# FP4 feed-forward in a four-layer kernel: levels from the rounded bit pattern, the sign put back as a bit

## The chip, the cores and the metric

One Trainium2 chip; the program runs on 1 of its cores. The metric is the device time of one execution in microseconds (us), as the median over several executions.

## The reference, cut to what matters

The whole program is four transformer-like layers, each with an attention-like stage and a feed-forward stage, on 16 sequences of 256 tokens with 128 features. The change touches only the feed-forward stage of the first layer, where tokens, weights and the gated hidden values are quantized to FP4 and back, in blocks of 16 along the last dimension:

```python
def fp4_quant_dequant(x):
    """Blockwise FP4 (E2M1) quantize + dequantize along the last dim."""
    shape = x.shape
    xb = x.reshape(shape[:-1] + (shape[-1] // BLOCK, BLOCK))
    scale = jnp.max(jnp.abs(xb), axis=-1, keepdims=True) / 6.0
    scale = jnp.maximum(scale, jnp.float32(1e-12))
    xn = xb / scale
    idx = jnp.searchsorted(_MID, jnp.abs(xn))
    q = _GRID[idx] * jnp.sign(xn) * scale
    return q.reshape(shape)
```

`_GRID` is 0, 0.5, 1, 1.5, 2, 3, 4, 6 and `_MID` holds the seven midpoints 0.25, 0.75, 1.25, 1.75, 2.5, 3.5, 5. Around it stand a layer norm with modulation, the products with `w_gate`, `w_up` (352 by 128) and `w_down` (128 by 352), a SiLU, and a gated residual.

## The kernel before, in words

`build_program` runs ten stages one after the other, with a barrier between them: a load, `stage_mamba`, `stage_fp4_ffn`, six further stages, and a store. All engines execute instruction lists written out by hand; semaphores join them.

`stage_fp4_ffn` works on B = 16 items, one sequence of 256 tokens each. It first normalizes all of x in 8 steps of two sequences (`AdaNorm`: TensorE centres and averages, ScalarE squares and takes the logarithm and exponential, VectorE multiplies, L287, and modulates, L290). Between these steps VectorE quantizes all weights in one go (`weight_step`; the quantizer `qw`, 128 by 1120 elements): it issues one piece of the work before each normalization step, and what is left after the eighth. TensorE then turns the weights, and the items follow.

There are three quantizers: `qw` for the weights, `qx` for the tokens of an item (128 by 256) and `qh` for its gated hidden values (128 by 704). In each, `Quantizer.act` (ScalarE) makes `mag` with Abs (L707) and `sign` with Sign (L708); `Quantizer.pool` (GpSimd) multiplies `sign` by half the block's scale (L714); and `Quantizer.dve` (VectorE) takes the block maximum (L732), scale, half scale and reciprocal (L734 to L736), normalizes `mag` by a product with the reciprocal, which is broadcast over the 16 elements of a block (L738), and counts the midpoints that are exceeded, in nine instructions (L741 to L753). The product of level and signed half scale (L758) is the result. `done` puts a semaphore wait behind every step that the next one reads; L734 and L735 and the reciprocal have no wait between L735 and L736.

The order of VectorE for item n is written in `item`: `hidden(n)` (gate by up, L990), `quantize_tokens(n + 1)`, `residual(n - 1)` (L298) and `quantize_hidden(n)`. TensorE does `back(n - 1)` (six transposes of the quantized hidden values, L896, between which ScalarE copies, L956, and six products with `w_down`, L901), then `project(n + 1)` (L881, L887, L888), then the transpose of the tokens of n + 2 (L859). ScalarE copies, quantizes its part and applies SiLU (L950). GpSimd copies the normalized tokens of n + 2 to a fixed place (`fixed`, L834) and makes the two products of L714. `residual(n - 1)` waits for `back(n - 1)`, and `back(n - 1)` waits for `quantize_hidden(n - 1)`, the last thing of the item before.

Of the kernel before, what the change touches and what calls it, by code (L numbers as in the profile page):

```python
# [8 lines left out]
P = 128  # L9
ALU = mybir.AluOpType  # L10
# [4 lines left out]
I32 = mybir.dt.int32  # L15
# [669 lines left out]
class Quantizer:  # L685
# [4 lines left out]
    STEPS = 11  # L690

    def __init__(self, core, sb, sg, name, blocks):
        self.nc, self.sg, self.name = core.nc, sg, name
        self.amax = sb(name + "_amax", [P, blocks, 1])
        self.scale = sb(name + "_scale", [P, blocks, 1])
        self.half = sb(name + "_half", [P, blocks, 1])
        self.mag = sb(name + "_mag", [P, blocks, 16])
        self.sign = sb(name + "_sign", [P, blocks, 16])
        self.level = sb(name + "_level", [P, blocks, 16])
        self.blocks = blocks  # L700

    def act(self, act, n, src, ready):

        nc, sg, name = self.nc, self.sg, self.name
        act.wait_ge(ready, n + 1)
        wait(act, sg[name + "_done"], n)
        nc.scalar.activation(self.mag[:, :, :], src, ACT.Abs).then_inc(sg[name + "_mag"], 1)  # L707
        nc.scalar.activation(self.sign[:, :, :], src, ACT.Sign).then_inc(sg[name + "_sign"], 1)  # L708

    def pool(self, pool, n):  # L710
        sg, name = self.sg, self.name
        pool.wait_ge(sg[name + "_sign"], n + 1)
        pool.wait_ge(sg[name + "_half"], n + 1)
        pool.tensor_tensor(self.sign[:, :, :], self.sign[:, :, :], self.half[:, :, :].to_broadcast([P, self.blocks, 16]),  # L714
                           ALU.mult).then_inc(sg[name + "_signed"], 1)

    def dve(self, dve, n, src, dst, read=0):
# [18 lines left out]
        done(nc.vector.reciprocal(self.amax[:, :, :], self.scale[:, :, :]))  # L736
# [3 lines left out]
        dve.wait_ge(sg[name + "_half"], n + 1)  # L740
        done(nc.vector.tensor_scalar(flat(self.level), flat(self.mag), 5.0, 2.0, ALU.is_gt, ALU.mult))  # L741
        yield
        for mid in (3.5, 2.5):
            done(nc.vector.scalar_tensor_tensor(out=flat(self.level), in0=flat(self.mag), scalar=mid, in1=flat(self.level),
                                                op0=ALU.is_gt, op1=ALU.add))
            yield
        done(nc.vector.tensor_scalar(flat(self.level), flat(self.level), 2.0, None, ALU.mult))
        yield
        for mid in (1.75, 1.25, 0.75):
            done(nc.vector.scalar_tensor_tensor(out=flat(self.level), in0=flat(self.mag), scalar=mid, in1=flat(self.level),  # L750
                                                op0=ALU.is_gt, op1=ALU.add))
            yield
        nc.vector.scalar_tensor_tensor(out=flat(self.level), in0=flat(self.mag), scalar=0.25, in1=flat(self.level),  # L753
                                       op0=ALU.is_gt, op1=ALU.add).then_inc(sg[name + "_level"], 1)
        dve.wait_ge(sg[name + "_level"], n + 1)
        dve.wait_ge(sg[name + "_signed"], n + 1)
        wait(dve, sg[name + "_taken"], read)
        nc.vector.tensor_tensor(dst, self.level[:, :, :], self.sign[:, :, :], ALU.mult).then_inc(sg[name + "_done"], 1)  # L758
# [3 lines left out]
def stage_fp4_ffn(core, T):  # L762
# [7 lines left out]
    with ExitStack() as ctx:  # L770
# [56 lines left out]
        def _(pool):  # L827
# [8 lines left out]
            def first():  # L836
                qw.pool(pool, 0)
                pool.wait_ge(sg["h"], B // 2)
                fixed(0, 0)
                fixed(1, 1)  # L840
                qx.pool(pool, 0)

            def item(n, j, nxt=2):
                if nxt == 2:
                    fixed(n + 2, j)
                if nxt:
                    qx.pool(pool, n + 1)
                qh.pool(pool, n)
# [131 lines left out]
        def _(dve):  # L980
# [6 lines left out]
            def hidden(n):  # L987
                dve.wait_ge(sg["silu"], n + 1)
                wait(dve, sg["qh_sign"], n)
# [2377 lines left out]
```

## Time and profile before

| What | us |
|---|---|
| three runs, median (lowest to highest) | 5523.27 (5519.79 to 5526.17) |
| the profiled execution's own time | 5521.02 |
| its span in the profile | 5519.3 |
| VectorE busy in the span | 3922.5 (71%) |
| TensorE busy in the span | 4929.2 (89%) |
| GpSimd busy in the span | 2660.5 (48%) |
| ScalarE busy in the span | 3359.4 (61%) |

The profile is one execution, with its instructions timed engine by engine. Its span lies 1.7 us under the time of its own execution, and that one 2.3 us under the median. The feed-forward stage that the change touches lies between about 563 and 919 us of the span. An average over the span tells nothing of it; the stage has to be read alone.

### The profile page before, as it was taken

The numbers are of one execution on the slowest core, as the hardware profiler recorded it, in microseconds if no ns is written. First come the engines' busy times: TensorE is split into PE (matmuls) and PEld (weight loads), VectorE is DVE, ScalarE is ACT, GpSimd is POOL, SyncE is SP. The second block draws the span as 40 slices with busy tenths as digits, with TensorE's granted clock in tenths as the row PEclk, the third lists the DMA queues.
The fourth block names the chain that finished last, engine by engine and source line by source line (L and its number), as shares of the span: only waits on it lengthen the run. The fifth ranks groups of instructions, "written<-read, shape, count | busy, mean of one in ns | idle before, by whom it ended". The sixth has DMA issues, their size and how long they took to land. (4 is left out here: it accounts for less than half of the span.)

```text
span 5519.3 us, 130512 instructions
## 1 busy us (share of the span) xinstructions
PE 4929.2 (89%) x50569; PEld 3352.3 (61%) x50569; DVE 3922.5 (71%) x6510; ACT 3359.4 (61%) x5923; POOL 2660.5 (48%) x1681
## 2 busy tenths in 40 slices
PE   6888555997899999999999999999999999799897
PEld 4444233554677667776777677766776777566544
DVE  5999797775677777777777677767777777477553
ACT  5776322554666666666666666666666666455444
POOL 4777110000566556665666566655555666266200
PEclk8999656998999999999999999999999999899898
DMA  2121000000000100010000000010001000000020
GB/s 84 61 77 62 4 0 7 2 1 19 17 12 12 29 14 11 11 30 15 11 11 20 25 11 11 12 30 12 11 11 33 12 11 11 14 2 2 24 62 19
DMA packets 76242, 113.90 MB, mean 21 GB/s; under 512 B 22496, under 2 KB 53424, under 8 KB 72048
## 3 DMA queue, kind: packets, MB, share of 16 engines
q1 hardware_dynamic: 67744, 110.60, 7.3%
q8 instruction: 157, 2.57, 0.2%
q10 hardware_dynamic: 8256, 0.03, 0.1%
q14 instruction: 85, 0.70, 0.0%
HBM read 70.38 MB, written 2.49 MB: 13 GB/s over the span
## 5 line engine op out<-in xcount | busy, mean ns | idle before, releaser
L2211 POOL TENSOR_TENSOR lt_qk<-lt_qk,lt_rot 128x1024 f32<-128x1024 f32 x384 | 907.0, 2362 | 207.3 <-DVE lt_rot L2575 207.3
L2221 POOL TENSOR_TENSOR lt_prob<-lt_prob,lt_total 128x1024 f32<-128x1024 f32 x192 | 365.1, 1902 | 1086.5 <-DVE lt_total L2597 1086.5
L2216 POOL TENSOR_TENSOR lt_qk<-lt_qk,lt_rnorm 128x1024 f32<-128x1024 f32 x384 | 726.2, 1901 | 110.5 <-ACT lt_rnorm L2451 102.9
L2258 PE MATMUL lt_ps<-lt_w_qk,lt_xs 128*128 128x512 f32 x1536 | 749.8, 611 | 23.0 <-DMA lt_scales<-in_L_scales 11.3
L2310 PE MATMUL lt_ps<-lt_z,lt_fold 128*128 128x256 f32 x3072 | 678.8, 379 | 1.3 <-ACT lt_z L2479 1.3
L2310 PEld LDWEIGHTS lt_ps<-lt_z,lt_fold 128*128 128x128 f32 x3072 | 583.6, 190 | 121.5 <-ACT lt_z L2479 24.4
L2572 DVE TENSOR_TENSOR lt_qk<-lt_ps,lt_table 128x1024 f32<-128x1024 f32 x384 | 467.8, 1218 | 79.0 <-ACT lt_sq L2441 72.1
L2575 DVE TENSOR_TENSOR lt_rot<-lt_ps,lt_table 128x512 f32<-128x512 f32 x768 | 490.1, 679 | 0.0
L2587 DVE TENSOR_REDUCE lt_nmax<-lt_ps 128x16 f32<-128x1024 f32 x192 | 229.9, 1197 | 360.5 <-PE lt_ps L2278 360.4
L2582 DVE TENSOR_REDUCE lt_norm<-lt_sq 128x16 f32<-128x1024 f32 x384 | 463.4, 1207 | 0.0
L2258 PEld LDWEIGHTS lt_ps<-lt_w_qk,lt_xs 128*128 128x128 f32 x1536 | 272.7, 193 | 253.9 <-issue 247.2
L2441 ACT ACTIVATE lt_sq<-lt_ps 128x1024 f32<-128x1024 f32 x384 | 393.2, 1024 | 50.9 <-PE lt_ps L2258 44.3
L2301 PEld LDWEIGHTS lt_ps<-lt_probT,lt_xw 64*128 64x128 f32 x3072 | 295.7, 187 | 175.2 <-issue 87.1
L2462 ACT ACTIVATE lt_prob<-lt_prob 128x1024 f32<-128x1024 f32 x192 | 203.2, 1058 | 320.2 <-DVE lt_prob L2590 320.2
L2265 PE MATMUL lt_ps<-ident,lt_qk 128*128 128x128 f32 x3072 | 389.9, 275 | 8.8 <-DVE lt_rot L2575 7.9
L2301 PE MATMUL lt_ps<-lt_probT,lt_xw 64*128 64x256 f32 x3072 | 385.1, 389 | 12.6 <-ACT lt_probT L2467 3.4
L2479 ACT COPY lt_z<-lt_ps 128x1024 f32<-128x1024 f32 x384 | 380.1, 1016 | 22.9 <-PE lt_ps L2301 21.7
L2265 PEld LDWEIGHTS lt_ps<-ident,lt_qk 128*128 128x128 f32 x3072 | 348.2, 142 | 37.8 <-DVE lt_rot L2575 8.8
L2846 POOL TENSOR_TENSOR mb_drive<-mb_u,mb_bs 128x1024 f32<-128x1024 f32 x128 | 301.2, 2359 | 84.6 <-DVE mb_state L3057 79.2
L3057 DVE TENSOR_TENSOR_SCAN mb_state<-mb_decay,mb_drive 128x1024 f32<-128x1024 f32 x128 | 292.2, 2283 | 20.4 <-POOL mb_drive L2846 19.3
L2278 PE MATMUL lt_ps<-lt_kT,lt_qT 64*32 64x64 f32 x24576 | 287.6, 225 | 14.3 <-issue 14.3
L2278 PEld LDWEIGHTS lt_ps<-lt_kT,lt_qT 64*32 64x32 f32 x24576 | 254.9, 105 | 59.5 <-issue 59.5
(406 smaller groups left out, 9935.5 us busy)
## 6 DMA issues: line engine op xcount, KB each, us to landing
mb_bs<-mb_rows SPq DMA_DIRECT2D x16, 1536.0 KB, 7.6
lt_xw<-lt_xw SPq DMA_DIRECT2D x192, 128.0 KB, 2.3
mb_bs<-mb_rows SPq DMA_DIRECT2D x16, 512.0 KB, 4.2
mo_gate_b<-mo_rows SPq DMA_DIRECT2D x16, 512.0 KB, 5.5
lt_xs<-h SPq DMA_DIRECT2D x96, 64.0 KB, 1.9
lt_w_qk<-in_L_ffn_Wqkv SPq DMA_DIRECT2D x6, 1024.0 KB, 4.9
lt_xs<-h SPq DMA_DIRECT2D x96, 63.8 KB, 1.9
lt_wvT<-in_L_wvT SPq DMA_DIRECT2D x6, 512.0 KB, 7.4
```

The costliest lines, as they stand in the source:

```text
L2211: pool.tensor_tensor(qk[:, u, :, :], qk[:, u, :, :], rot[:, u % 2, :, :], ALU.add).then_inc(sg["added"], 1)
L2216: pool.tensor_tensor(qk[:, u, :, :], qk[:, u, :, :], rnorm[:, u, :, :].to_broadcast([P, H, DH]), ALU.mult).then_inc(sg["qk"], 1)
L2258: last = pe.matmul(AT[u][:, 512 * k:512 * k + 512], xs[:, m.j, c:c + P], w_qk[:, a, 512 * k:512 * k + 512], start=True, stop=True)
L2265: last = pe.transpose(to[:, P * g:P * g + P], qk[:, u, 2 * g:2 * g + 2, :].rearrange("p a b -> p (a b)"), core.ident[:, :])
L2278: last = pe.matmul(to[WIN * w:WIN * w + WIN, 512 * k + 64 * g:512 * k + 64 * g + 64], qT[r:r + 64, g, c:c + WIN], kT[r:r + 64, g, c:c + 2 ...
L2301: last = pe.matmul(to[:, c:c + 256], xw[r:r + 64, copy, i_w, :], probT[r:r + 64, t, :, WIN * w:WIN * w + WIN], start=True, stop=True, tile ...
L2310: last = pe.matmul(attn, fold[:, slot // 8, slot % 8, :], z[:, k, :, i, :], start=(slot == 0), stop=(slot == H - 1))
L2441: nc.scalar.activation(sq[:, u % 2, :], AT[u], ACT.Square).then_inc(sg["square"], 1)
L2479: act.copy(dst, src.rearrange("p (k c) -> p k c", k=2)).then_inc(sg["z"], 1)
L2572: nc.vector.tensor_tensor(qk[:, u, :, :], src, table[:, t, a, 0, :, :].to_broadcast([P, H, DH]), ALU.mult)
L2575: last = nc.vector.tensor_tensor(rot[:, u % 2, :, HD * k:HD * k + HD], src[:, :, HD * (1 - k):HD * (1 - k) + HD], table[:, t, a, 1, :, HD ...
L2582: nc.vector.tensor_reduce(norm[:, u, :], sq[:, u % 2, :].rearrange("p (h d) -> p h d", h=H), AX.X, ALU.add).then_inc(sg["sumsq"], 1)
```

## The change

The quantizer works out the same values in another way. Sign on ScalarE (L708) and the product on GpSimd (L714) are gone, and with them the tile `sign`. VectorE divides by half the scale instead of the scale, for which the reciprocal now waits for the half. It finds the level by cutting the exponent out of the bit pattern (a bitwise AND on an int32 view), adding a quarter of it to the value, and cutting the sum to its upper bits (a second AND); two comparisons give the correction for the small levels. The level is then multiplied by the half scale, broadcast over the block, and the last instruction takes the sign bit of the source with AND and joins it with OR. This last instruction reads the source, so `hidden(n)` now waits until `quantize_hidden(n - 1)` is done, where it waited for the Sign of ScalarE. A new tile `low` takes the place of `sign`.

```diff
-    STEPS = 11
+    STEPS = 10
...
-        nc.scalar.activation(self.sign[:, :, :], src, ACT.Sign).then_inc(sg[name + "_sign"], 1)
-
-    def pool(self, pool, n):
-        sg, name = self.sg, self.name
-        pool.wait_ge(sg[name + "_sign"], n + 1)
-        pool.wait_ge(sg[name + "_half"], n + 1)
-        pool.tensor_tensor(self.sign[:, :, :], self.sign[:, :, :], self.half[:, :, :].to_broadcast([P, self.blocks, 16]),
-                           ALU.mult).then_inc(sg[name + "_signed"], 1)
...
         nc.vector.tensor_scalar(self.half[:, :, :], self.scale[:, :, :], 0.5, None, ALU.mult).then_inc(sg[name + "_half"], 1)
-        done(nc.vector.reciprocal(self.amax[:, :, :], self.scale[:, :, :]))
+        dve.wait_ge(sg[name + "_half"], n + 1)
+        done(nc.vector.reciprocal(self.amax[:, :, :], self.half[:, :, :]))
         dve.wait_ge(sg[name + "_mag"], n + 1)
         done(nc.vector.tensor_tensor(self.mag[:, :, :], self.mag[:, :, :], self.amax[:, :, :].to_broadcast(shape), ALU.mult))
         yield
-        dve.wait_ge(sg[name + "_half"], n + 1)
-        done(nc.vector.tensor_scalar(flat(self.level), flat(self.mag), 5.0, 2.0, ALU.is_gt, ALU.mult))
+        bits = flat(self.level).bitcast(I32)
+        done(nc.vector.tensor_scalar(bits, flat(self.mag).bitcast(I32), 0x7F800000, None, ALU.bitwise_and))
         yield
-        for mid in (3.5, 2.5):
-            done(nc.vector.scalar_tensor_tensor(out=flat(self.level), in0=flat(self.mag), scalar=mid, in1=flat(self.level),
-                                                op0=ALU.is_gt, op1=ALU.add))
-            yield
-        done(nc.vector.tensor_scalar(flat(self.level), flat(self.level), 2.0, None, ALU.mult))
+        done(nc.vector.scalar_tensor_tensor(out=flat(self.level), in0=flat(self.level), scalar=0.25 - 2.0 ** -23, in1=flat(self.mag),
+                                            op0=ALU.mult, op1=ALU.add))
         yield
-        for mid in (1.75, 1.25, 0.75):
-            done(nc.vector.scalar_tensor_tensor(out=flat(self.level), in0=flat(self.mag), scalar=mid, in1=flat(self.level),
-                                                op0=ALU.is_gt, op1=ALU.add))
-            yield
-        nc.vector.scalar_tensor_tensor(out=flat(self.level), in0=flat(self.mag), scalar=0.25, in1=flat(self.level),
-                                       op0=ALU.is_gt, op1=ALU.add).then_inc(sg[name + "_level"], 1)
+        done(nc.vector.tensor_scalar(bits, bits, 0x7FC00000, None, ALU.bitwise_and))
+        yield
+        done(nc.vector.tensor_scalar(flat(self.low), flat(self.mag), 1.5, -2.0, ALU.is_gt, ALU.add))
+        yield
+        done(nc.vector.scalar_tensor_tensor(out=flat(self.low), in0=flat(self.mag), scalar=0.5, in1=flat(self.low),
+                                            op0=ALU.is_gt, op1=ALU.add))
+        yield
+        nc.vector.scalar_tensor_tensor(out=flat(self.level), in0=flat(self.level), scalar=2.0, in1=flat(self.low),
+                                       op0=ALU.max, op1=ALU.add).then_inc(sg[name + "_level"], 1)
         dve.wait_ge(sg[name + "_level"], n + 1)
-        dve.wait_ge(sg[name + "_signed"], n + 1)
+        done(nc.vector.tensor_tensor(self.level[:, :, :], self.level[:, :, :], self.half[:, :, :].to_broadcast(shape), ALU.mult))
+        yield
         wait(dve, sg[name + "_taken"], read)
-        nc.vector.tensor_tensor(dst, self.level[:, :, :], self.sign[:, :, :], ALU.mult).then_inc(sg[name + "_done"], 1)
+        nc.vector.scalar_tensor_tensor(out=dst.bitcast(I32), in0=src.bitcast(I32), scalar=-2 ** 31, in1=self.level[:, :, :].bitcast(I32),
+                                       op0=ALU.bitwise_and, op1=ALU.bitwise_or).then_inc(sg[name + "_done"], 1)
...
             def first():
-                qw.pool(pool, 0)
                 pool.wait_ge(sg["h"], B // 2)
                 fixed(0, 0)
                 fixed(1, 1)
-                qx.pool(pool, 0)
 
             def item(n, j, nxt=2):
                 if nxt == 2:
                     fixed(n + 2, j)
-                if nxt:
-                    qx.pool(pool, n + 1)
-                qh.pool(pool, n)
...
-                wait(dve, sg["qh_sign"], n)
+                wait(dve, sg["qh_done"], n)
                 nc.vector.tensor_tensor(hid[:, :, :], gate[:, :, :], ps_u[:, :, 0:I], ALU.mult).then_inc(sg["hid"], 1)
```

The pieces of the weight quantizer are fewer now, and one more of them falls between the normalization steps. VectorE at the end of the normalization, before the change (L750, L753 and L758 are pieces of `qw`, L287 and L290 the last normalization steps):

```order
191 L287 TENSOR_TENSOR h<-cen,rstd 128x512
192 L290 TENSOR_SCALAR h<-h,mod 128x256 x2
193 L750 SCALAR_TENSOR_TENSOR fp_qw_level<-fp_qw_mag,fp_qw_level 128x1120
194 L287 TENSOR_TENSOR h<-cen,rstd 128x512
195 L290 TENSOR_SCALAR h<-h,mod 128x256 x2
196 L750 SCALAR_TENSOR_TENSOR fp_qw_level<-fp_qw_mag,fp_qw_level 128x1120
197 L753 SCALAR_TENSOR_TENSOR fp_qw_level<-fp_qw_mag,fp_qw_level 128x1120
198 L758 TENSOR_TENSOR fp_wraw<-fp_qw_level,fp_qw_sign 128x1120
```

And the same place with the change, with the changed kernel's own line numbers:

```order
191 L287 TENSOR_TENSOR h<-cen,rstd 128x512
192 L290 TENSOR_SCALAR h<-h,mod 128x256 x2
193 L746 SCALAR_TENSOR_TENSOR fp_qw_level<-fp_qw_level,fp_qw_low 128x1120
194 L749 TENSOR_TENSOR fp_qw_level<-fp_qw_level,fp_qw_half 128x1120
195 L287 TENSOR_TENSOR h<-cen,rstd 128x512
196 L290 TENSOR_SCALAR h<-h,mod 128x256 x2
197 L752 SCALAR_TENSOR_TENSOR fp_wraw<-fp_wraw,fp_qw_level 128x1120
198 L724 TENSOR_REDUCE fp_qx_amax<-fp_h_tok 128x16
```

Behind the last normalization step three pieces of `qw` stood; one stands there now.

## Rows read from the trace of the kernel before

**Rows 1.** Stretch, busy us of PE, PEld, DVE, ACT, POOL; granted clock, DMA

```profile
617.20:892.60 275.40, 149.57 (x346) 80.91 (x346) 259.02 (x450) 67.83 (x147) 43.10 (x43) 0.62 0.00 0
```

**Rows 2.** VectorE in order of time, one item: start us, us, engine, line, operation

```profile
707.82 0.89 DVE L758 TENSOR_TENSOR fp_hidq<-fp_qh_level,fp_qh_sign 128x704 f32<-128x704 f32 x1
...
714.75 0.42 DVE L758 TENSOR_TENSOR fp_hq<-fp_qx_level,fp_qx_sign 128x256 f32<-128x256 f32 x1
715.31 0.48 DVE L298 SCALAR_TENSOR_TENSOR x<-fp_ps_o,mod,x 128x256 f32 x1
...
716.85 0.18 DVE L735 TENSOR_SCALAR fp_qh_half<-fp_qh_scale 128x44 f32<-128x44 f32 x1
716.94 0.42 DVE L736 RECIPROCAL fp_qh_amax<-fp_qh_scale 128x44 f32<-128x44 f32 x1
717.40 1.91 DVE L738 TENSOR_TENSOR fp_qh_mag<-fp_qh_mag,fp_qh_amax 128x704 f32<-128x704 f32 x1
...
726.19 0.89 DVE L758 TENSOR_TENSOR fp_hidq<-fp_qh_level,fp_qh_sign 128x704 f32<-128x704 f32 x1
```

**Rows 3.** One group of VectorE: duration ns min/median/max, first and last start us

```profile
L758 DVE TENSOR_TENSOR fp_hidq<-fp_qh_level,fp_qh_sign x16: 891/892/893, 634.0 to 909.9; 128x704 f32<-128x704 f32 x16
```

**Rows 4.** TensorE in order of time, the same item

```profile
708.77 0.69 PE L896 MATMUL fp_ps_t<-ident,fp_hidq 128*128 128x128 f32 x2 [6.26 <-DVE fp_hidq L758]
...
712.19 2.93 PE L901 MATMUL fp_ps_o<-fp_hidT,fp_wd 128*128 128x256 f32 x6 [0.46 <-ACT fp_hidT L956]
```

**Rows 5.** Who waited for whom, VectorE, 604 to 920 us: in total, times, longest

```profile
DVE x L298 <- PE fp_ps_o L901: 13.8, 8, 6.5
```

**Rows 6.** ScalarE in order of time: the SiLU of the next item

```profile
721.48 0.76 ACT L950 ACTIVATE fp_gate<-fp_ps_g 128x704 f32<-128x704 f32 x1 [5.15 <-PE fp_ps_u L888]
```

**Rows 7.** Groups of VectorE by form: count, busy us, mean ns, idle before

```profile
L750 DVE SCALAR_TENSOR_TENSOR fp_qh_level<-fp_qh_mag,fp_qh_level 128x704 f32<-128x704 f32 x48 | 42.8, 892 | 1.6
...
L738 DVE TENSOR_TENSOR fp_qh_mag<-fp_qh_mag,fp_qh_amax 128x704 f32<-128x704 f32 x16 | 30.5, 1908 | 0.5
...
L738 DVE TENSOR_TENSOR fp_qx_mag<-fp_qx_mag,fp_qx_amax 128x256 f32<-128x256 f32 x16 | 13.7, 857 | 0.5
...
L741 DVE TENSOR_SCALAR fp_qh_level<-fp_qh_mag 128x704 f32<-128x704 f32 x16 | 9.4, 587 | 0.6
...
L747 DVE TENSOR_SCALAR fp_qh_level<-fp_qh_level 128x704 f32<-128x704 f32 x16 | 8.4, 527 | 0.5
...
L753 DVE SCALAR_TENSOR_TENSOR fp_qx_level<-fp_qx_mag,fp_qx_level 128x256 f32<-128x256 f32 x16 | 6.8, 426 | 0.6
...
L750 DVE SCALAR_TENSOR_TENSOR fp_qw_level<-fp_qw_mag,fp_qw_level 128x1120 f32<-128x1120 f32 x3 | 3.9, 1316 | 0.0
...
L738 DVE TENSOR_TENSOR fp_qw_mag<-fp_qw_mag,fp_qw_amax 128x1120 f32<-128x1120 f32 x1 | 2.9, 2896 | 0.0
...
L741 DVE TENSOR_SCALAR fp_qw_level<-fp_qw_mag 128x1120 f32<-128x1120 f32 x1 | 0.7, 735 | 0.0
```

**Rows 8.** GpSimd in order of time, beside L738 of rows 2

```profile
717.17 1.38 POOL L714 TENSOR_TENSOR fp_qh_sign<-fp_qh_sign,fp_qh_half 128x704 f32<-128x704 f32 x1 [6.15 <-DVE fp_qh_half L735]
```

**Rows 9.** A group of VectorE with a broadcast operand in a later stage

```profile
L2590 DVE TENSOR_TENSOR lt_prob<-lt_ps,lt_nmax 128x1024 f32<-128x1024 f32 x192 | 235.0, 1224 | 14.1
```

**Rows 10.** All engines, normalization and weights, in order of time

```profile
570.99 1.12 ACT L708 ACTIVATE fp_qw_sign<-fp_wraw 128x1120 f32<-128x1120 f32 x1
...
577.64 0.69 DVE L287 TENSOR_TENSOR h<-cen,rstd 128x512 f32<-128x512 f32 x1 [6.37 <-ACT rstd L278]
...
600.40 2.86 POOL L834 COPY fp_h_fixed<-h 128x256 f32<-128x256 f32 x2 [18.71 <-DVE h L290]
...
604.36 0.41 DVE L732 TENSOR_REDUCE fp_qx_amax<-fp_h_tok 128x16 f32<-128x256 f32 x1
```

**Rows 11.** Groups of GpSimd by form: the copy of the tokens, here and in a later stage

```profile
L834 POOL COPY fp_h_fixed<-h 128x256 f32 x12 | 12.7, 1060 | 0.0
...
L1839 POOL COPY ca_h_fixed<-h 128x256 f32 x14 | 5.6, 400 | 40.6 <-PE ca_ps_s L1866 40.6
```

More of the change, by code:

```diff
@@ L697, in __init__ @@
         self.mag = sb(name + "_mag", [P, blocks, 16])
-        self.sign = sb(name + "_sign", [P, blocks, 16])
         self.level = sb(name + "_level", [P, blocks, 16])
+        self.low = sb(name + "_low", [P, blocks, 16])
         self.blocks = blocks
```

## The prediction

> **What bounds the kernel now.** The change lies in one stage, so I read that stretch alone. First the busy times by stretch: over items 0 to 14 (617.2 to 892.6 us) VectorE is busy 259.0 of 275.4 us (94%), TensorE 54%, ScalarE 25%, GpSimd 16%, and TensorE's granted clock is 0.62, which means most of the time its lower level (1.2 of 2.4 GHz) [rows 1]. VectorE is the bound, nearly. Then the order of time of one item, to see how near. Call t the end of the quantized hidden values (L758, 707.82 + 0.89 = 708.71). The next such end is at 727.08, so an item takes 18.37 us; over all 16 items the mean is the same, 275.9 us in 15 periods, 18.39 [rows 3]. Inside it VectorE finishes the tokens of the next item at 715.17 and starts the residual (L298) at 715.31, t + 6.60; from there to the end of the hidden values it needs 11.77 [rows 2]. TensorE meanwhile starts its transposes at 708.77, and the last product that the residual reads ends at 712.19 + 2.93 = 715.12, t + 6.41 [rows 4]. So both inputs of the residual arrive within 0.05 us of each other. The waits show the same from the other side: in 8 cases the residual waited for that product, at most 6.5 us [rows 5]. This is the number that decides most: what VectorE saves **before** the residual runs into TensorE's chain, which hangs on t too; what it saves **behind** it shortens every item. SiLU of the next item ends at 722.24, 4.8 us before VectorE wants it [rows 6], so the chain through the gate has room.
>
> **Prices.** A VectorE instruction with two tensor inputs costs 892 ns at 704 elements, 426 at 256, 1316 at 1120; one with a single input costs 527 at 704 and 735 at 1120 [rows 7], and about 293 at 256 by the same line (157 ns and two elements per cycle of 0.96 GHz). The product L738 stands out: 1908, 857 and 2896 ns. That looks like the price of its broadcast operand, but isn't. GpSimd's product runs from 717.17 to 718.55 and L738 from 717.40 to 719.31 [rows 2, 8]; from the end of GpSimd's to that of VectorE's are 0.76 us, and 704 elements at one per cycle are 0.73. VectorE stood still until GpSimd was through. And a broadcast operand with no GpSimd beside it costs 1224 ns for 1024 elements, one element per cycle and 157 ns [rows 9]. So without L714 the product L738 should cost 892, 426 and 1316, and the added product with the half scale the same.
>
> **Hidden values, behind the residual.** Before, from L738 to the result: 1908 + 2 x 527 + 7 x 892 = 9206 ns (L738, two single-input steps, seven with two). After: 892 (L738) + 3 x 527 (two ANDs and one comparison) + 3 x 892 + 892 (broadcast product) + 892 (sign) = 6933. That is 2.27 less, and one instruction less takes its gap of 0.04 with it. The reciprocal now waits for the half: it started 0.09 us after the start of the half and 0.09 before its end; behind a wait the next instruction starts 0.04 after the end (L736 to L738) [rows 2], so this costs 0.13. Net 2.18 us per item, all 16 items: **34.9 us**. The Trainium skill, "VectorE: DVE Perf Modes", section on the DRAIN, says that a semaphore after each operation costs nothing extra; by it the sum would gain 2.1 us. The rows show an overlap that the wait takes away, and I go by them.
>
> **Tokens, ahead of the residual.** Before 857 + 2 x 293 + 7 x 426 = 4425, after 426 + 3 x 293 + 5 x 426 = 3435; with the gap and the wait 0.99 + 0.04 - 0.12 = 0.91 us less. `hidden` now waits for the end of L758, where it could overlap it, for another 0.12 at most. In items 1 to 15 all of this is worth nothing: VectorE would be ready at about t + 5.8, TensorE's product is not there before t + 6.4, and the residual starts at t + 6.6 as before. The saving becomes a wait of some 0.8 us. Only the tokens of item 0 and those of item 1, in front of which no residual stands, count: **1.8 us**.
>
> **Normalization and weights.** ScalarE's Sign of the weights (1.12 us) lies ahead of its part of the normalization, for which VectorE idles 6.37 us until 577.64 [rows 10]: 1.1 us earlier. From there VectorE is nearly full. Its weight work falls by 1.58 (L738 without GpSimd), and behind it from 2 x 735 + 7 x 1316 = 10.68 to 3 x 735 + 5 x 1316 = 8.79 us, with 0.13 for the reciprocal's wait and 0.04 for the gap: 3.4 us. Of these 4.5 us I count 3.6: the tokens of item 0 hang on a GpSimd copy and a transpose behind the last normalization step, and the copy that started at 600.40 and the one behind it took 2.86 us beside VectorE [rows 10]. **3.6 us.**
>
> **At nothing.** ScalarE's two Signs per item: ScalarE is busy a quarter of the time and the Abs that VectorE reads comes well before. GpSimd's two products: nobody waits for them but VectorE; the copy of the tokens loses its place behind them and comes earlier. It took 1060 ns here and 400 in a later stage [rows 11], as it waits for VectorE, while the VectorE step behind it was 0.06 us longer than its like (587 against 527) [rows 7]; I keep that cost as it is, at another step. The Trainium skill, "SBUF — State Buffer", section on the two sides, has a lock: whichever of GpSimd and such a VectorE instruction starts first holds the ports for all of it. If the copy won each time, VectorE would stand up to 0.4 us in 16 items instead of 0.06, and the sum would be 5 us worse; the rows show the copy as the one that waits.
>
> **Sum.** 34.9 + 1.8 + 3.6 = 40.3 us. The profiled execution took 5521.0, so 5480.7; the median of the runs is 2.3 above it: **5483**.
>
> **Open prices.** No row shows a bitwise instruction. The two ANDs are bounded below by 527 and above by 892, the price of one element per cycle; I take 527, since they are of the form of L741 and L747 (one tensor in SBUF, an immediate). At 892 the hidden values lose 0.73 per item (11.7 us), weights and first tokens 1.7 more. The sign instruction reads two tensors like L750, 892; I find no reason for less. All three could also be slower than any row, which is rival C.
>
> **Rivals.**
>
> A. *The ANDs run at one element per cycle.* For it: nothing shows integer data at two per cycle. Against: the form of the instruction. 5483 + 13.4 = 5496. By the Trainium skill, "Vector Engine (DVE) Microarchitecture Reference", section on performance modes, the two-port mode depends on SBUF and an even size, not on type, which speaks for 527.
>
> B. *TensorE's chain gets shorter too.* The items come closer, TensorE's share rises from 54% to about 62%, and if its granted clock were at the upper level during L896 and L901, the residual would wait no more and the 0.9 us of the tokens would count in 14 items: 12.6 us more, 5470. Against: the granted clock of 0.62 [rows 1], and that in this chain of transposes, copies and products nothing gets denser. The Trainium skill, "TensorE: Matmul & The Clock Gate", part 1, has the clock rise with TensorE's recent activity, which is this rival's mechanism.
>
> C. *Slower: bitwise instructions on 32-bit integers take two cycles per element.* Then an AND of 704 costs 1624 ns and the sign 1624: 2.93 us more per item, 46.8 in 16; in the tokens 1.07, of which the wait of 0.9 hides most (about 4 us in all), and in the weights 4.7. That is 55.6 over the forecast: 5539, slower by 15 us. It decides from about 1.7 cycles per element on, where the extra cost reaches 40 us. Against: no instruction of VectorE in this profile is that slow once GpSimd's share is taken out.
>
> D. *The broadcast costs double in itself* and the overlap with GpSimd is chance. Then L738 stays at 1908 and the new product costs 1908 too: 0.15 us per item, with the weights some 4 us in all: 5519, no change. The change would then have saved GpSimd's work and nothing else. Against: the broadcast product that stands alone [rows 9], and how exactly the ends fit.
>
> **Chances.** Forecast 0.70, A 0.12, B 0.10, C 0.05, D 0.03. A measurement of this kernel tells 0.2%, 11 us, from no change: forecast, A and B are faster (0.92), D the same (0.03), C slower (0.05). The range reaches from B to A with a few us for the clock's phase in the stages behind, which run the same work at other moments: 5467 to 5502. C and D are left out, with 0.08.
>
> **What would show it.** L738 at 892, 426 and 1317 ns; the ANDs at 527 and 293; the two products with a broadcast alike; a period of about 16.2 us; the residual waiting for TensorE in nearly every item, 0.6 to 0.9 us each, with L298 still at t + 6.6; the first tokens' reduction (604.36 before [rows 10]) 3 to 4.5 us earlier. The forecast is wrong if L738 is still near 1900, if an AND costs more than 900, or if the residual starts well before t + 6.4.

## The result and the profile after

| What | before | after |
|---|---|---|
| median of the runs side by side, 4 of each (us) | 5521.53 | 5470.35 |
| lowest to highest | 5517.36 to 5526.17 | 5467.04 to 5471.46 |
| ratio of the times | | 0.991 (0.9895 to 0.9925) |
| the profiled execution, own time and span | 5521.02, 5519.3 | 5470.79, 5469.0 |
| feed-forward stage | 347.32 | 307.07 |
| next two stages | 429.4 | 429.1 |
| local transformer stage | 3433.8 | 3422.8 |
| everything behind it | 738.8 | 739.4 |

The time fell by 51 us to 5470.35, inside the range (5467 to 5502), 13 below the predicted 5483. The lower half of the table cuts the span at fixed instructions of the program: the stage runs from the start of VectorE's reduction of the weights to the start of its last residual, the local transformer from one of GpSimd's fills at its beginning (`lt_kT`) to one at the beginning of the next stage (`gq_nmax`). The changed stage gave 40.25 us, against 40.3 forecast. Another 11.0 came from the local transformer, whose code is the same.

First the busy times of the changed kernel by stretch, the columns as in [rows 1]. The stretch is 15 periods of 16.17 us:

```profile
615.00:857.50 242.50, 144.06 (x350) 81.48 (x350) 214.48 (x419) 53.01 (x117) 8.17 (x12) 0.64 0.00 0
```

VectorE is busy 88% of it, where it was 94% [rows 1]; GpSimd's 43.10 us have become 8.17. TensorE's granted clock is 0.64 after 0.62. That is a mean over everything TensorE does there; in the chain that the residual waits for it is lower, as the next views show.

VectorE in order of time, one item (start us, us, engine, line, operation, idle time before it and what ended it):

```profile
692.10 0.89 DVE L752 SCALAR_TENSOR_TENSOR fp_hidq<-fp_hid,fp_qh_level 128x704 int32<-128x704 int32 x1
693.10 0.89 DVE L980 TENSOR_TENSOR fp_hid<-fp_gate,fp_ps_u 128x704 f32<-128x704 f32 x1
...
698.34 0.43 DVE L752 SCALAR_TENSOR_TENSOR fp_hq<-fp_h_tok,fp_qx_level 128x256 int32<-128x256 int32 x1
699.60 0.48 DVE L298 SCALAR_TENSOR_TENSOR x<-fp_ps_o,mod,x 128x256 f32 x1 [0.84 <-PE fp_ps_o L891]
...
701.13 0.19 DVE L727 TENSOR_SCALAR fp_qh_half<-fp_qh_scale 128x44 f32<-128x44 f32 x1
701.35 0.43 DVE L729 RECIPROCAL fp_qh_amax<-fp_qh_half 128x44 f32<-128x44 f32 x1
701.81 0.89 DVE L731 TENSOR_TENSOR fp_qh_mag<-fp_qh_mag,fp_qh_amax 128x704 f32<-128x704 f32 x1
702.74 0.53 DVE L734 TENSOR_SCALAR fp_qh_level<-fp_qh_mag 128x704 int32<-128x704 int32 x1
...
708.29 0.89 DVE L752 SCALAR_TENSOR_TENSOR fp_hidq<-fp_hid,fp_qh_level 128x704 int32<-128x704 int32 x1
```

The quantized hidden values are ready at 692.99 and again at 709.18. The residual L298 starts at 699.60, 6.61 us after the first, as before [rows 2], though the tokens are now done at 698.77. From the residual to the result it is 9.58 us, where it was 11.77. TensorE's part hangs on the same event and kept its length:

```profile
693.05 0.69 PE L886 MATMUL fp_ps_t<-ident,fp_hidq 128*128 128x128 f32 x2 [4.24 <-DVE fp_hidq L752]
...
696.47 2.93 PE L891 MATMUL fp_ps_o<-fp_hidT,fp_wd 128*128 128x256 f32 x6 [0.46 <-ACT fp_hidT L946]
```

The last product ends at 699.40, 6.41 after the result, the same number as in [rows 4]. The closer items did not bring TensorE's upper level (2.4 GHz) to this chain: its granted clock is 0.50 here (first row below, columns as in [rows 1]), the lower level. Behind the very first result, at 628.68, it was 0.61 (second row); there the chain took 5.91 us and the residual started 5.95 after the result.

```profile
692.99:699.40 6.41, 4.97 (x13) 3.06 (x14) 5.26 (x15) 1.80 (x4) 0.00 (x0) 0.50 0.00 0
628.68:634.60 5.92, 4.49 (x13) 2.59 (x14) 5.25 (x14) 1.80 (x4) 0.00 (x0) 0.61 0.00 0
```

What VectorE saved ahead of the residual has become idle time (who waited for whom, VectorE, 590 to 880 us):

```profile
DVE x L298 <- PE fp_ps_o L891: 23.8, 16, 6.5
```

Of these 23.8 us the residuals of the last two items hold 12.0, where they held 12.2 of the 13.8 before [rows 5]; the new waiting lies in the other items.

The groups of VectorE by form give the prices (count, busy us, mean ns, idle before), to be held against [rows 7]:

```profile
L746 DVE SCALAR_TENSOR_TENSOR fp_qh_level<-fp_qh_level,fp_qh_low 128x704 f32<-128x704 f32 x16 | 14.6, 915 | 0.5
...
L749 DVE TENSOR_TENSOR fp_qh_level<-fp_qh_level,fp_qh_half 128x704 f32<-128x704 f32 x16 | 14.3, 896 | 0.5
L752 DVE SCALAR_TENSOR_TENSOR fp_hidq<-fp_hid,fp_qh_level 128x704 int32<-128x704 int32 x16 | 14.3, 892 | 1.7
L731 DVE TENSOR_TENSOR fp_qh_mag<-fp_qh_mag,fp_qh_amax 128x704 f32<-128x704 f32 x16 | 14.3, 892 | 0.6
...
L739 DVE TENSOR_SCALAR fp_qh_level<-fp_qh_level 128x704 int32<-128x704 int32 x16 | 8.6, 536 | 0.5
...
L734 DVE TENSOR_SCALAR fp_qh_level<-fp_qh_mag 128x704 int32<-128x704 int32 x16 | 8.4, 527 | 0.5
```

The product with the reciprocal fell from 1908 to 892 ns in the same form; what changed beside it is GpSimd's product, which is gone. The first experiment puts that back. The ANDs L734 and L739 cost what one tensor and an immediate cost in float: with 293 ns at 256 elements (measured below) they take 0.52 ns per element, half the 1.04 of an instruction with two tensors (892 and 425). The integer AND-OR L752 costs what any instruction with two tensors costs.

### The profile page after: what moved, and what is told of

Same layout as the page of the kernel before. It is cut to its first block and busy times, and to the rows that moved or that the text cites. A ratio compares the mean times of both kernels' runs of the same rounds, so it can differ in the third digit from the quotient of the medians.

```text
span 5469.0 us, 130315 instructions
## 1 busy us (share of the span) xinstructions
PE 4913.4 (90%) x50569; PEld 3348.9 (61%) x50569; DVE 3873.2 (71%) x6477; ACT 3344.0 (61%) x5890; POOL 2620.7 (48%) x1648
## 5 line engine op out<-in xcount | busy, mean ns | idle before, releaser
L2248 PE MATMUL lt_ps<-lt_w_qk,lt_xs 128*128 128x512 f32 x1536 | 744.6, 608 | 21.6 <-DMA lt_scales<-in_L_scales 11.8
L2291 PE MATMUL lt_ps<-lt_probT,lt_xw 64*128 64x256 f32 x3072 | 383.6, 388 | 11.8 <-ACT lt_probT L2457 2.3
```

What stands on the lines that cost most here:

```text
L2248: last = pe.matmul(AT[u][:, 512 * k:512 * k + 512], xs[:, m.j, c:c + P], w_qk[:, a, 512 * k:512 * k + 512], start=True, stop=True)
L2291: last = pe.matmul(to[:, c:c + 256], xw[r:r + 64, copy, i_w, :], probT[r:r + 64, t, :, WIN * w:WIN * w + WIN], start=True, stop=True, tile ...
```

## The experiments

All of them start from the changed kernel, unless said otherwise. Period means the mean distance between quantized hidden values over 15 items; the stage is measured as in the table. Where no number of runs is given, the stage and period are of the one profiled run. Repeats stand beside their first run.

### The product back on GpSimd, on a tile that nobody reads

Is it GpSimd that made the product with the reciprocal slow? GpSimd multiplies an otherwise unused tile by the half scale, at the old places; VectorE's last instruction also waits for it.

```diff
+        self.aside = sb(name + "_aside", [P, blocks, 16])
...
+        pool.wait_ge(sg[name + "_half"], n + 1)
...
+        pool.tensor_tensor(self.aside[:, :, :], self.aside[:, :, :], self.half[:, :, :].to_broadcast([P, self.blocks, 16]),
+                           ALU.mult).then_inc(sg[name + "_signed"], 1)
```

> The changed kernel, with GpSimd's products put back on a tile of their own that nobody uses (same sizes, same wait for the half scale, VectorE's last instruction waits for them). Lock theory: the product L738/L731 of VectorE, which starts 0.2 us behind GpSimd's, stands still until that ends, so it is back at about 1908, 857 and 2896 ns where it is 892, 425 and 1326 in the changed kernel; all else of VectorE stays. The stage (first reduction of the weights to the last residual, 307.1 us in the changed kernel, 347.3 before) gets 16 x 1.02 + 2 x 0.43 + 1.6 = 19 us longer, 326 us. Rival, the product was dear for another reason (its place, its operands): it stays at 892 and the stage at 307.

Measured: stage 324.29 us (+17.2), period 17.07; the one run took 5498.78. GpSimd and then VectorE at the place in question, two views of one stretch:

```profile
707.76 1.38 POOL L715 TENSOR_TENSOR fp_qh_aside<-fp_qh_aside,fp_qh_half 128x704 f32<-128x704 f32 x1 [5.97 <-issue]
```

```profile
707.66 0.43 DVE L738 RECIPROCAL fp_qh_amax<-fp_qh_half 128x44 f32<-128x44 f32 x1
708.12 1.77 DVE L740 TENSOR_TENSOR fp_qh_mag<-fp_qh_mag,fp_qh_amax 128x704 f32<-128x704 f32 x1
```

GpSimd ends at 709.14, VectorE's product at 709.89: 0.75 us later, the time that 704 elements take at 1.04 ns each (0.73 us), though it started at 708.12. So the product's data moved only after GpSimd had ended. The mean is 1769 ns, not 1908, because the reciprocal's wait starts it 0.36 us behind GpSimd and not 0.23; that is the miss of about 2 us against the expectation.

The repeat, timed in 4 runs:

> e1_product_aside again, with more runs. Its stage is 17.2 us longer than the changed kernel's. If nothing else differs, its runs lie 17 us above c2_after_again within 3. In its first profile the local transformer stage took 3434.1 us, as before the change; if GpSimd's products in this stage lengthen a later one in some way, the distance is 24 us or more.

Median 5489.57, ratio to before 0.995 (0.9934 to 0.9967). That is 18.4 above the changed kernel beside it, for a stage that is 18.0 longer (324.35 against 306.39).

### GpSimd busy, but reading nothing

Against the kernel before this one, the product aside:

```diff
-        pool.tensor_tensor(self.aside[:, :, :], self.aside[:, :, :], self.half[:, :, :].to_broadcast([P, self.blocks, 16]),
-                           ALU.mult).then_inc(sg[name + "_signed"], 1)
+        pool.memset(self.aside[:, :, :], 1.0).then_inc(sg[name + "_signed"], 1)
```

> As e1_product_aside, but GpSimd only fills the unused tile with a constant at the same moment, so it writes and reads nothing. If what stops VectorE is GpSimd's reading, the products of VectorE stay at 892 and 425 ns and the stage at 307 us. If writing is enough, a fill of 704 elements (about 0.65 us by the 1031 ns for 1120) that starts 0.2 us ahead holds VectorE for some 0.45 us, the product is at 1.3 us and the stage at about 315 us.

Measured: stage 306.74, as without it (the whole run, 5480.02, is 9 us longer; 5.3 of that stand in the next two stages, with 434.4). The two engines again, GpSimd's row first:

```profile
701.49 0.68 POOL L715 MEMSET fp_qh_aside<- 128x704 f32 x1 [6.27 <-DVE fp_qh_half L735]
```

```profile
701.88 0.89 DVE L739 TENSOR_TENSOR fp_qh_mag<-fp_qh_mag,fp_qh_amax 128x704 f32<-128x704 f32 x1
```

They overlap for 0.29 us and the product takes its 0.89. So a GpSimd that is busy does not by itself hold VectorE: its product does, which reads two tiles, and its fill doesn't, which reads none. The Trainium skill, "SBUF — State Buffer", section "SBUF: two separate sides", says of a VectorE operation with two inputs in SBUF: it contends only against a GpSimd operation that reads SBUF, and the one that comes second waits for all of the first. Both runs agree; that it is the reading, and not another difference between a product and a fill, rests on that page.

### Which half of the change pays

The old levels with the new sign: seven comparisons in eight instructions as before (L741 to L753; they were counted as nine above), then the broadcast product and the sign bit on VectorE; no Sign, no GpSimd product. Against before:

```diff
-        dve.wait_ge(sg[name + "_signed"], n + 1)
+        done(nc.vector.tensor_tensor(self.level[:, :, :], self.level[:, :, :], self.half[:, :, :].to_broadcast(shape), ALU.mult))
...
-        nc.vector.tensor_tensor(dst, self.level[:, :, :], self.sign[:, :, :], ALU.mult).then_inc(sg[name + "_done"], 1)
+        nc.vector.scalar_tensor_tensor(out=dst.bitcast(I32), in0=src.bitcast(I32), scalar=-2 ** 31, in1=self.level[:, :, :].bitcast(I32),
+                                       op0=ALU.bitwise_and, op1=ALU.bitwise_or).then_inc(sg[name + "_done"], 1)
```

> The kernel before with one half of the change: no Sign, no GpSimd product; the level of nine steps as before, then VectorE multiplies it by the half scale and joins the sign bit. Theory: VectorE gets back what it stood still behind GpSimd (1908 to 892 per item) and pays it out again for its own product (892) and a further gap, and `hidden` can no longer overlap the end of the item before: the stage stays at 347 us within 2 (347.3 before), so this half is worth nothing by itself. Rival, that freeing GpSimd is what pays: the stage falls by 16 us or more, to 331 or less.

> k7_sign_only again, with more runs. Its stage is 2.5 us shorter than before the change (344.8 for 347.3). If nothing else differs its runs lie 2 to 3 us under those of the kernel before; if taking Sign and GpSimd's products away shortens the stages behind, 8 us or more under.

Measured: stage 344.83 and 344.78 us, 2.5 below before, a little more than the 2 expected; 1.1 of it lie ahead of the first tokens, where ScalarE's Sign of the weights is gone. Period 18.32. Ten runs: 5509.52, ratio 0.9982 (0.9973 to 0.9992), 10 us less than before (5519.75 beside it), of which the stage explains a quarter; the rest is taken up below.

And the new levels with the old sign (Sign on ScalarE, half scale on GpSimd, `level` by `sign` at the end):

```diff
-        done(nc.vector.tensor_tensor(self.level[:, :, :], self.level[:, :, :], self.half[:, :, :].to_broadcast(shape), ALU.mult))
...
-        nc.vector.scalar_tensor_tensor(out=dst.bitcast(I32), in0=src.bitcast(I32), scalar=-2 ** 31, in1=self.level[:, :, :].bitcast(I32),
-                                       op0=ALU.bitwise_and, op1=ALU.bitwise_or).then_inc(sg[name + "_done"], 1)
+        dve.wait_ge(sg[name + "_signed"], n + 1)
+        nc.vector.tensor_tensor(dst, self.level[:, :, :], self.sign[:, :, :], ALU.mult).then_inc(sg[name + "_done"], 1)
```

> The changed kernel with the old sign path: Sign on ScalarE and the product with the half scale on GpSimd, the new level of six steps on VectorE, and a plain product at the end. Theory: VectorE loses 0.88 us behind GpSimd in the product (1769 ns for 892, as in e1_product_aside) and saves its own product of 892: the stage stays within 1.5 us of the changed kernel's 307.1, so the shorter level is the whole gain. Rival, as in k7_sign_only: without freeing GpSimd most of the 40 us are gone again and the stage is over 320 us.

Measured: stage 307.72 us, within 0.7 of the changed kernel; the one run took 5473.64. The same view of groups, this kernel:

```profile
L740 DVE TENSOR_TENSOR fp_qh_mag<-fp_qh_mag,fp_qh_amax 128x704 f32<-128x704 f32 x16 | 28.5, 1778 | 0.6
```

VectorE pays 0.886 us here for GpSimd's company and would pay 0.892 for the broadcast product. Whatever the change says of GpSimd and Sign, nearly all of the stage's gain (39.6 of 40.25 us) is the shorter chain of levels; the product on VectorE costs as much as GpSimd's product cost VectorE.

### The residual behind the hidden values

If the tokens' saving is lost to TensorE's chain, a different order must win it back:

```diff
-                if not fresh(n):
-                    residual(n - 1)
                 quantize_hidden(n)
+                if not fresh(n):
+                    residual(n - 1)
```

> The changed kernel with the residual of item n - 1 behind the quantization of the hidden values of item n, where it stood ahead of it. Theory that TensorE's chain ahead of the residual eats what the tokens saved: the 0.8 us wait in each item goes, the period falls from 16.2 to about 15.35 us (14 items, 11 us) and in item 15 the wait of 5.5 us goes too: some 17 us in all, the stage at about 290 us and the time at about 5453. Rival, the wait is hidden behind something else that then ends last (the gate's chain over TensorE and SiLU, which is ready at t + 13.5): the period stays near 16 and at most the 5.5 us go.

Measured: stage 287.24 us (-19.8, some 17 expected), period 14.83; 5454.26 in 4 runs, ratio 0.9879 (0.9863 to 0.9896). Only the last residual still waits (VectorE, 590 to 880 us), and in the loop it stands hard against its neighbours:

```profile
DVE x L298 <- PE fp_ps_o L891: 6.1, 1, 6.1
```

```profile
702.42 0.89 DVE L752 SCALAR_TENSOR_TENSOR fp_hidq<-fp_hid,fp_qh_level 128x704 int32<-128x704 int32 x1
703.23 0.48 DVE L298 SCALAR_TENSOR_TENSOR x<-fp_ps_o,mod,x 128x256 f32 x1
703.62 0.88 DVE L980 TENSOR_TENSOR fp_hid<-fp_gate,fp_ps_u 128x704 f32<-128x704 f32 x1
```

The period shrinks by 1.34 us in the mean, unevenly. The last of the 15 distances falls by 4.4 us, from 15.92 to 11.48: its residual had waited 5.5. The other 14 fall by 1.1 each, from 16.19 to 15.07: the wait of 0.84 to 0.99 and some 0.2 of gaps, since the residual starts 0.08 before the end of L752 and L980 0.09 before the residual's. Expected were 0.8 for each of these and 5.5 for the last.

The same with the half scale computed straight from the block maximum, one small instruction fewer on the chain of each quantizer:

```diff
-        done(nc.vector.tensor_scalar(self.scale[:, :, :], self.amax[:, :, :], 1.0 / 6.0, 1e-12, ALU.mult, ALU.max))
-        nc.vector.tensor_scalar(self.half[:, :, :], self.scale[:, :, :], 0.5, None, ALU.mult).then_inc(sg[name + "_half"], 1)
+        nc.vector.tensor_scalar(self.half[:, :, :], self.amax[:, :, :], 1.0 / 12.0, 5e-13, ALU.mult, ALU.max).then_inc(sg[name + "_half"], 1)
```

> e3_residual_late, and the half scale computed straight from the block maximum (one twelfth of it, lower bound 5e-13), so that the scale's own instruction goes. VectorE ends last in every item of e3_residual_late (period 14.83 us), so each of the two instructions saved per item, 0.19 and 0.17 us with a gap of 0.04, counts in full: period 14.4, stage 287.2 - 7 = 280 us, time 34 us under c2_after_again. Rival, the gate's chain (ready 13.5 us behind the hidden values) or the Abs of ScalarE becomes what ends last: the stage stays above 284.

Measured: 5442.73 in 4 runs (5439.81 to 5446.00), ratio 0.986 (0.9844 to 0.9877): faster than both kernels, 28.5 below the changed one beside it. Expected were 34 below and a stage of 280. Stage 277.73, period 14.35, another 0.48 per item (most of it the scale with its gap, 0.22 in the hidden values and 0.21 in the tokens, which now count in every item). The stage alone gives 28.7 against the changed kernel's repeat.

### Where the other 11 us are

The stages behind differ though their code is the same. One thought was the moment at which they start; a chain of memsets ahead of the weights delays it and leaves the rest alone (32 of them here; 10 in the first try):

```diff
+            for pad in range(32):
+                pool.memset(wraw[:, :, :], 0.0).then_inc(sg["w_pad"], 1)
+                pool.wait_ge(sg["w_pad"], pad + 1)
             pool.memset(wraw[:, :, :], 0.0).then_inc(sg["w_zero"], 1)
```

> The changed kernel with ten more fills of the weight tile by GpSimd ahead of the stage's first load, each waited for: a plain delay of about 11 us, nothing else. It tells where the 11 us come from that the local transformer stage (unchanged code) is shorter with the change: 3433.7 us from its first fill to that of the next stage before, 3422.8 with the change. If it is a matter of where TensorE's spells at the lower clock happen to fall (85 us of them in that stage before, 68 with the change), the length moves with the delay, anywhere between about 3418 and 3438, and the total is not simply 5470 + 11 = 5481. If it comes with the change itself (its code or its tiles), the length stays at 3423 within 1 us and the total is 5481.

> The changed kernel with 32 fills ahead of the stage: a plain delay of about 40 us, so that everything behind the stage starts at the moment at which it did before the change. If the moment of the start decides where the spells fall, the local transformer stage is 3434 us long again and the total 5521. If it is chance in each execution, the length lies anywhere from 3423 to 3436, and the four totals scatter about 5510 to 5515. If the code decides, the length is 3423 and the total 5511.

Ten memsets: the stage starts 12.6 us later, 5477.13 in 4 runs (5472.25 to 5482.92), 6.8 above the changed kernel's first median and 4 below the 5481 of a plain delay; the local transformer takes 3423.5. Thirty-two: 33.7 later than in the kernel's repeat, so that the local transformer starts at 1344.5, where it does in before (1346.7). It takes 3426.8, neither the 3434 of before nor the 3423 that the first profile had. Ten runs: 5505.59, ratio 0.9978 (0.9968 to 0.9987), 34.4 above the changed kernel's repeat, below every time that was expected (5510 to 5521). So the delay is paid about once and the 11 us do not come back with it: not the start.

The unchanged kernel and the changed one again:

> The kernel before, unchanged: how far do its runs and its local transformer stage scatter by themselves? If chance spells of TensorE's lower clock make the difference there, a second profile gives another length, somewhere from 3423 to 3436 us (3433.8 in the first), and the totals scatter by some 10 us. If the length belongs to the code, it is 3433.8 within 1 us again.

> The changed kernel, unchanged, in as many runs as the kernel before beside it. The stage explains 40.2 us of the difference. If the rest of the 51 us that the first four runs showed was chance, the difference of the means is 40 us within 3 here; if the stages behind are really shorter with the change, it stays at 46 or more. Its local transformer stage: 3423 us if that belongs to the code, elsewhere up to 3431 if it scatters.

The unchanged kernel: 5515.25 in 10 runs, ratio to itself 0.9994 (0.9984 to 1.0003), local transformer 3430.8. The changed: 5471.19 in 4 runs, ratio 0.9917 (0.99 to 0.9933), local transformer 3422.9. Beside runs of before taken with them, the changed kernel's medians lie 51 and 49 us lower, 8 to 11 beyond the stage; against the unchanged kernel's ten runs, taken at another time, it is 44, 4 beyond. The stage alone would be a ratio of 0.9927, just outside the first interval (to 0.9925) and inside the second: the medians alone hardly show more than the stage. The two pairs of profiles do, with a local transformer 11.0 and 7.9 us shorter.

The profiles show two things that differ. **The first is the program's own**: places where VectorE or ScalarE wait for nothing that the profile shows ("issue"). Who waited for whom in the local transformer, before, VectorE and ScalarE:

```profile
DVE lt_xn L2612 <- issue: 4.5, 1, 4.5
...
DVE lt_qk L2572 <- issue: 4.3, 1, 4.3
DVE lt_b_up L2677 <- issue: 2.0, 1, 2.0
DVE lt_hid L2620 <- issue: 2.0, 1, 2.0
...
DVE lt_total L2595 <- issue: 0.2, 1, 0.2
```

```profile
ACT lt_log L2448 <- issue: 3.5, 1, 3.5
...
ACT lt_gel L2497 <- issue: 2.8, 2, 2.3
...
ACT lt_xw L2473 <- issue: 1.4, 1, 1.4
...
ACT lt_probT L2467 <- issue: 0.9, 1, 0.9
```

And all rows of that kind after:

```profile
DVE lt_total L2585 <- issue: 4.8, 2, 3.4
DVE lt_qk L2562 <- issue: 4.5, 2, 4.3
```

```profile
ACT lt_gel L2487 <- issue: 0.9, 1, 0.9
```

That is 21.6 us before and 10.2 after. The second profile of each has the same rows within 0.1 us, but for L2595 (gone), L2585 (5.1 and not 4.8) and L2487 (2.3 and not 0.9): 21.2 and 11.9. The delayed kernel has the rows of the changed one (11.8 us); the kernel with the old sign has 12.7, the one with the new sign alone 5.9 to 7.3. So these stops stand at fixed places of a program and move when instructions of an earlier stage come or go. One of them can be followed. ScalarE in order of time, before and after, the same item:

```profile
3581.78 1.00 ACT L2441 ACTIVATE lt_sq<-lt_ps 128x1024 f32<-128x1024 f32 x1
3583.66 1.01 ACT L2467 COPY lt_probT<-lt_ps 128x1024 f32<-128x1024 f32 x1 [0.87 <-issue]
```

```profile
3538.68 1.00 ACT L2431 ACTIVATE lt_sq<-lt_ps 128x1024 f32<-128x1024 f32 x1
3539.59 1.00 ACT L2457 COPY lt_probT<-lt_ps 128x1024 f32<-128x1024 f32 x1
```

From VectorE's L2590 of this item to that of the next one are 29.85 us before (3579.56 to 3609.41); the same stretch after takes 29.02 (3536.46 to 3565.48): 0.83 lost to a stop of 0.87. Taken together the stops cost less than they last. If the stage is cut at every second L2590, the stretches that differ between before and after by a stop, and not by TensorE's clock, add up to 1.0 of the 11.0 us, and the longest stop (L2612, 4.5 us) stands in a stretch that is 1.3 us longer than its counterpart in this pair and 1.1 shorter in the repeated one. The stretches that differ by the clock alone give 5.9. And the kernel with the new sign alone, with the fewest stops, took 3425.9 and 3430.3 us here: no run shows that stops make the stage longer as a whole.

**The second is TensorE's clock.** It runs at its lower level for 85 us of this stage before and 68 after, in pieces at the stage's start and end and near the borders between its six parts of 32 items, mostly soon after TensorE was idle: in before it stood idle for 11.3 us up to 1378.6, and the longest piece of the start, 13.7 us, begins at 1370.5, within that. More than half of the difference, 5.7 us, lies behind the last L2590, where before has 20.5 us at the lower level and 4.3 of stops and after has 7.0 and 0.9 (in the repeats 3.6 us, with 20.6 and 4.3 against 15.6 and 2.3). Away from there eight items take 137.1 to 137.4 us in every kernel. Over the 14 profiles the lower level lasts 68 to 89 us and the stage 3422.8 to 3434.1, each us more at the lower level going with 0.4 to 0.5 us more of stage. It differs between executions of one program: the product aside had 89 us and 3434.1, its repeat 68 and 3426.8. A straight line of length against time at the lower level, through the 12 profiles of other code than before's, puts before's two 2.7 and 1.0 us above it, while those 12 lie between 3.2 below and 3.0 above: once the clock is taken out, nothing clear of the scatter is left for the stops. Why before's two profiles have more of the lower level than the changed kernel's two (85 and 82 us against 68 and 68) no run tells; the kernel with 32 memsets, which starts the stage where before does, has 78.

## Why the prediction was right, point by point

- **What bounds the kernel**: right. The residual starts 6.6 or 6.8 us after the hidden values in most items of both kernels, in turns, and the period shrank by 2.22 us with 2.19 saved behind the residual. The exception is the first distance, 15.45 us where it was 18.11: TensorE's clock was in part at the upper level there and the residual came at 5.95, about 0.5 us early.
- **Prices**: right. L731 at 892, 425 and 1326 ns (892, 426, 1316 forecast); the ANDs at 527 and 536, 293, and 734 to 745; the sign at 892. Rivals A (ANDs at 892) and C (1624) are gone, and D with them: the broadcast costs nothing by itself, and it is GpSimd's product that held VectorE, as the two runs with work aside show.
- **Hidden values, 34.9 us**: right. 11.77 less 9.58 are 2.19 per item, 2.18 forecast. The reciprocal starts 0.22 after the start of the half, where it started 0.09: the 0.13 of the wait. The Trainium skill, "VectorE: DVE Perf Modes", section on the DRAIN, counts a semaphore behind each operation at nothing, which would have given 2.1 us more; the rows (0.22 against 0.09) disagree with it for this short instruction.
- **Tokens, 1.8 us**: right that only items 0 and 1 count. The wait of 0.8 forecast is 0.84 to 0.99, and the late residual wins it back. These two terms together measure 37.2 us (40.25 less the next one), against 36.7; the 0.5 more is the first distance.
- **Normalization and weights, 3.6 us**: 3.0. The reduction of the first tokens starts 31.41 us after the stage's begin, where it was 34.41 [rows 10]. VectorE itself gained what was forecast: 1.0 us up to the first L287 (7.69 to 6.66) and 3.5 from there to the end of the weights (26.79 to 23.25), 4.6 in all for 4.5. What was mis-sized is the deduction of 0.9 for the chain through the GpSimd copy and the transpose: the first tokens are ready 2.70 us after the last L290 in both kernels, VectorE has only one piece of weight work (1.32) to fill that time, and waits 1.5. A stop without a recorded cause isn't the reason, as both kernels have one among the weights (VectorE, in order of time, before, then after):

```profile
589.91 1.32 DVE L744 SCALAR_TENSOR_TENSOR fp_qw_level<-fp_qw_mag,fp_qw_level 128x1120 f32<-128x1120 f32 x1 [0.66 <-issue]
```

```profile
588.12 0.74 DVE L739 TENSOR_SCALAR fp_qw_level<-fp_qw_level 128x1120 int32<-128x1120 int32 x1 [0.64 <-issue]
...
602.06 0.42 DVE L724 TENSOR_REDUCE fp_qx_amax<-fp_h_tok 128x16 f32<-128x256 f32 x1 [1.50 <-ACT fp_h_tok L919]
```

- **At nothing**: the two copies at the start took 1.76 us where they took 2.86, and a copy that falls beside L743 or L746 still costs that step 0.08 to 0.16 us in most cases (mean 907 and 915 against 892).
- **The sum**: 40.3 forecast, 40.25 in the stage. That it fits to 0.1 is luck in part: 0.6 too much for the weights and 0.5 too little for the items cancel. The term that was off is the one that gave the stages behind "a few us for the clock's phase" in the range and nothing in the sum: they gave 11.0 in the profiled pair, 8 to 11 in the medians side by side, and with them the time lies 3 us above the lower end of the range. Nothing in the profile of before told the sign or the size of that. Rival B's time, 5470, came out, but not by its mechanism: the clock in the chain is 0.50, and L298 kept its place. The mechanism of B showed behind the first result alone to an amount that counts, about 0.5 us of its 12.6.

What stays open: why before spends more time at TensorE's lower level in the local transformer, whether the changed kernel's gain there would last over many executions, and what makes a stop. Two profiles of each kernel are few where two profiles of one program differ by 7 us. No run moved the stops alone, for instance by adding instructions that do nothing ahead of that stage, and the profile names no cause for them. The 5 to 8 us by which the new sign alone came out under before beyond its stage are not explained either.

## What to carry to other kernels

A two-input VectorE step that looks slow is first to be laid beside GpSimd's rows: if its end follows GpSimd's end by exactly its own data time, it stood still, and moving GpSimd's product to VectorE then costs nothing, though it also gains nothing. In a loop where two engines hang on one event, price a saving by its side of the meeting point: ahead of it it is idle time until the order is changed, as the late residual did for another 19.8 us of the stage. And hold a whole-program difference against the stage that was edited; in the profiled pair here a fifth of it came from stages that nobody touched.

## What the hardware showed that was not expected

- A memset of GpSimd (684 ns for 704 elements) beside a two-input product leaves it at 892 ns; a product of GpSimd holds it for all the overlap.
- Bitwise AND on int32 with an immediate costs 527 ns for 704 elements, like the float form; AND then OR on two int32 tensors 892.
- Engines stop for 0.2 to 4.5 us at places with no recorded cause, mostly the same to 0.1 us in two executions of one program and elsewhere after an edit in another stage; most of that time cost the stage nothing that could be measured.
- A stage of 3.4 ms scatters by 7 us between two profiles of one program, with the pieces in which TensorE runs at its lower level.
